# Routing, slots and scatter of two expert layers as one stage, zero rows written earlier, output stored by groups

## The reference, cut to what matters

```python
x = x + _L0_xattn_ref(_layernorm(x), ctx, ctx, ...)   # then L0_ffn, L1_xattn (performer)
x = x + _L1_ffn_ref(_layernorm(x, axis=-1), ...)      # 8 experts, two per row
x = x + _L2_xattn_ref(_layernorm(x), ctx, ctx, ...)   # keys of 16 heads x 64: ctx @ Wk
...                                                   # L2_ffn, L3_xattn
x = x + _L3_ffn_ref(_layernorm(x, axis=-1), ...)      # 8 experts, two per row

# the expert layers
logits = x @ Wg + bg                  # 8 logits a row
topk_vals, topk_idx = top_k(logits, 2)
weights = softmax(topk_vals)
out = sum of the two chosen experts' outputs, weighted
```

## Time and profile before

| | us |
|---|---|
| median of 3 runs | 3621.08 (3618.56 to 3623.73) |
| profiled execution | 3623.01 |
| its span | 3621.2 |
| L1f route and place | about 1380 to 1560 |
| L3f route and place | about 3131 to 3298 |
| last DVE instruction to the end | 15.7 |

### The profile page before, as it was taken

How to read it: one execution, slowest core, us unless ns; L and a number is a source line. 1 busy time by engine, 2 the same in 40 slices (tenths; PEclk the granted TensorE clock), 3 DMA queues, 4 the chain that set the end, 5 groups by cost and what they waited for, 6 DMA issues and landing times. The chain is left out here.

```text
span 3621.2 us, 73997 instructions
## 1 busy us (share of the span) xinstructions
PE 2969.1 (82%) x23917; PEld 2108.0 (58%) x23926; DVE 2351.7 (65%) x5338; ACT 1689.6 (47%) x2884; POOL 1213.0 (33%) x1311
## 2 busy tenths in 40 slices
PE   5997899999979996999959999984564999715980
PEld 4886222323227885889947777772343777515970
DVE  5887666666435657134458888859996898733653
ACT  3774788888934441423314444433443666300110
POOL 1112455555513441630013333320002777342005
PEclk9998899999989997999979999996786999857995
DMA  3000445445422004722232111100003333412224
GB/s 101 16 14 26 118 123 132 120 125 125 121 83 91 14 15 163 272 99 71 71 108 60 54 48 55 54 31 1 0 0 129 112 110 117 137 55 83 91 90 128
DMA packets 197370, 304.12 MB, mean 84 GB/s; under 512 B 23808, under 2 KB 134528, under 8 KB 191104
## 3 DMA queue, kind: packets, MB, share of 16 engines
q1 hardware_dynamic: 184816, 268.49, 24.1%
q0 software_dynamic: 12432, 34.10, 2.9%
HBM read 215.46 MB, written 78.64 MB: 81 GB/s over the span
## 5 line engine op out<-in xcount | busy, mean ns | idle before, releaser
L2308 ACT ACTIVATE params<-L0f_Z,params 128x1024 f32<-128x1024 f32 x512 | 532.6, 1113 | 84.0 <-PE L0f_Z L2364 83.8
L2285 POOL TENSOR_TENSOR L0f_mixed<-L0f_mixed,L0f_gated 128x512 f32<-128x512 f32 x240 | 332.0, 1383 | 291.7 <-DVE L0f_gated L2528 291.4
L2528 DVE SCALAR_TENSOR_TENSOR L0f_gated<-L0f_O,params 128x512 f32<-128x512 f32 x240 | 180.1, 750 | 223.9 <-PE L0f_O L2373 147.9
L2364 PE MATMUL L0f_Z<-params,L0f_w_stacked 128*128 128x512 f16 x1024 | 296.8, 388 | 34.1 <-ACT params L2308 23.3
L2373 PE MATMUL L0f_O<-params 128*32 128x512 f32 x2048 | 275.0, 609 | 0.4 <-ACT params L2308 0.4
L855 POOL TENSOR_TENSOR params<-params,L2x_recip_den 128x512 f32<-128x512 f32 x128 | 134.9, 1054 | 354.0 <-DVE L2x_recip_den L1110 353.6
L2364 PEld LDWEIGHTS L0f_Z<-params,L0f_w_stacked 128*128 128x128 f16 x1024 | 70.4, 98 | 289.9 <-ACT params L2308 266.2
L2008 ACT ACTIVATE L1ftiles_hidden<-L1ftiles_H,L1ftiles_b_tile 128x128 f32<-128x128 f32 x292 | 83.2, 368 | 196.3 <-PE L1ftiles_H L2031 196.3
L849 POOL DMA_INDIRECT L2x_gathered<-rows_out_dram,L1f_slots x64 | 63.8, 998 | 288.3 <-POOLq L136 256.3
L1554 DVE TENSOR_TENSOR L1x_products<-L1x_S,const_sb 128x512 f32<-128x512 f32 x128 | 82.5, 686 | 109.8 <-PE L1x_S L1464 109.8
L2031 PEld LDWEIGHTS L3ftiles_H<-L3ftiles_rowsT,L3ftiles_w_tile 128*128 128x128 f32 x1168 | 143.3, 195 | 7.4 <-DVE L3ftiles_rowsT L2059 2.0
(11 more groups left out here) (510 smaller groups left out, 7597.6 us busy)
## 6 DMA issues: line engine op xcount, KB each, us to landing
params<-gates_dram SPq DMA_DIRECT2D x512, 128.0 KB, 3.3
params<-side_dram SPq DMA_DIRECT2D x32, 1024.0 KB, 4.9
keysT_dram<-L1fplace_keysT SPq DMA_DIRECT2D x32, 512.0 KB, 3.4
params<-keysT_dram SPq DMA_DIRECT2D x32, 512.0 KB, 4.0
rows_in_dram<-L1froute_zero SPq DMA_DIRECT2D x2, 4864.0 KB
L1ftiles_rows<-rows_in_dram SPq DMA_DIRECT2D x76, 128.0 KB, 2.0
rows_in_dram<-L3froute_zero SPq DMA_DIRECT2D x2, 4864.0 KB
L3ftiles_rows<-rows_in_dram SPq DMA_DIRECT2D x76, 128.0 KB, 2.0
```

The lines of the kernel that those rows point to most:

```text
L2285: pool.tensor_tensor(acc[:, b.slot, m % KT, :], acc[:, b.slot, m % KT, :], tmp[:, m % 2, :], ALU.add).then_inc(mixed, 1)
L2308: act.activation(hid[:, n % 4, :, :], Z[:, n % 2, :, :], ACT.Gelu, bias=w["b1"][:, n // 4:n // 4 + 1]).then_inc(hid_ready, 1)
L2364: mm = pe.matmul(Z[:, n % 2, s, :], w1s[:, e, :], stack[:, b.slot, t, 2 * half + s, :], start=True, stop=True)
L2528: dve.scalar_tensor_tensor(out=out, in0=O[:, m % 2, :], scalar=w["b2"][:, e:e + 1], in1=gb[:, e % AHEAD, m % KT, :], op0=ALU.add, op1=ALU. ...
```

## The change

`route` and `place` become one stage, `prepare`. The norm's small steps are done once for all 32 batches instead of once for four. Routing goes in 16 turns of two batches; the rows' transposes of the next turn stand ahead of this turn's logits, and in L1f one key tile of L2x follows each turn from the fifth on (12 in all), four more stand ahead of the count. The applies write `kept` directly, so POOL's copies are gone. In L1f the gate's matmul takes 8 columns, in L3f 128 as before. The statistics of L1f's norm are taken in L1x, one instruction behind each `add_out`; those of L3f in its own stage. The zeros are written during L1x by 19 DMAs of four tiles, one behind a context load, and not at all before L3f. The key weights of L2x have a load and a semaphore of their own, issued second. The output is stored inside the combine stage, after each group of four batches.

```diff
--- before.py
+++ after.py
...
+    def load_columns(self, sp, phase, at, to, loaded):
+        sp.dma_start(self.stores[SIDE[phase]][:, at:to], self.dram["p_" + phase][:, at:to]).then_inc(loaded, 16)
...
-def last_stores(nc, sh):
-    stored = nc.alloc_semaphore("out_stored")
-    with nc.Block() as block:
-        @block.sync
-        def _(sp):
-            for q in range(4):
-                b = BATCH // 4
-                sp.dma_start(sh.dram["out"][q * b:(q + 1) * b].rearrange("b s d -> s b d"),
-                             sh.x[:, q * b:(q + 1) * b, :]).then_inc(stored, 16)
-            sp.wait_ge(stored, 64)
...
+        zero_set, zeroed, measured = core.sem("zero_set"), core.sem("slots_zeroed"), core.sem("rows_measured")
+        ZEROS, ZERO_TILES = 19, (SLOT_TILES + TILES_AHEAD) // 19
...
-            following(Turn(0, 2))
-            with sp.Fori(0, AHEAD) as i:
-                for s in (3, 4):
-                    following(Turn(i, s))
-            following(Turn(0, BATCH - 1))
+            tiles = sh.dram["rows_in"].rearrange("(j p) d -> p j d", p=P)
+            sp.wait_ge(zero_set, 1)
+            for b in range(2, BATCH):
+                following(Turn(0, b))
+                if 6 <= b < 6 + ZEROS:
+                    at = (b - 6) * ZERO_TILES
+                    sp.dma_start(tiles[:, at:at + ZERO_TILES, :],
+                                 zero[:, :].unsqueeze(1).broadcast_to([P, ZERO_TILES, D])).then_inc(zeroed, 16)
+            sp.wait_ge(zeroed, ZEROS * 16)
...
+            def measure(b):
+                dve.wait_ge(banks.emptied("proj"), banks.until_emptied("proj", b))
+                detach_wait(dve)
+                dve.bn_stats(sh.row_stats[:, b.n, :], sh.x[:, b.n, :]).then_inc(measured, 1)
...
                 if not first:
                     add_out(b.plus(-1))
+                    measure(b.plus(-1))
...
-        route(nc, sh, phase, w, c, kept, lg, rows_in, next_phase)
-        place(nc, sh, phase, c, lg[:, :, :], gate, slot, share, expert, kept, rows_in, next_phase)
+        prepare(nc, sh, phase, w, c, lg[:, :, :], gate, slot, share, expert, kept, rows_in, next_phase)
...
+def prepare(nc, sh, phase, w, c, lg, gate, slot, share, expert, kept, rows_in, next_phase):
...
+    E, G = 8, 2
...
+    measured = phase == "L1f"
+    keys_ahead = next_phase == "L2x"
+    LW = E if keys_ahead else P
...
+        xnT = core.sb("xnT", [P, KT, G * P])
+        X = core.ps("X", [P, 2, KT, G * P])
+        L = core.ps("L", [P, 2, BANK])
+        R, C = (X[:, k, :, :].rearrange("p k t -> p (k t)")[:, 0:BATCH * E] for k in range(2))
...
+        KEYS_FROM = 4
+        def keys_of(t):
+            return max(0, t - KEYS_FROM), max(0, t + 1 - KEYS_FROM)
+        ROUTE_KEYS = keys_of(TURNS)[0]
+        COUNT_KEYS = ROUTE_KEYS + 4
...
                 load(0)
+                sh.load_columns(sp, next_phase, KEY_COLUMNS, 2 * KEY_COLUMNS, wk_loaded)
                 load(1)
+                sh.loads[next_phase] = 32
+                for at in (0, 2 * KEY_COLUMNS):
+                    sh.load_columns(sp, next_phase, at, KEY_COLUMNS if at == 0 else columns(next_phase), sh.loaded[next_phase])
...
+            def empty_rows(t):
+                act.wait_ge(turned, t + 1)
+                if t:
+                    act.wait_ge(routed, t)
...
+            empty_rows(0)
+            for t in range(TURNS):
+                if t + 1 < TURNS:
+                    empty_rows(t + 1)
+                empty_keys(*keys_of(t))
...
+            def turn_rows(t):
+                pe.wait_ge(xn_ready, t + 1)
+                if t >= 2:
+                    pe.wait_ge(xT_ready, t - 1)
+                for k in range(KT):
+                    for j in range(G):
+                        mm = pe.transpose(X[:, t % 2, k, j * P:(j + 1) * P], kept[:, t * G + j, k * P:(k + 1) * P], c["ident"])
+                mm.then_inc(turned, 1)
+            def logits(t):
+                pe.wait_ge(xT_ready, t + 1)
+                if t >= 2:
+                    pe.wait_ge(logits_out, t - 1)
+                for j in range(G):
+                    for k in range(KT):
+                        mm = pe.matmul(L[:, t % 2, j * LW:(j + 1) * LW], xnT[:, k, j * P:(j + 1) * P], w["wg"][:, k, 0:LW],
+                                       start=(k == 0), stop=(k == KT - 1))
+                mm.then_inc(routed, 1)
+            def project_keys(first, end):
...
+            turn_rows(0)
+            for t in range(TURNS):
+                if t + 1 < TURNS:
+                    turn_rows(t + 1)
+                logits(t)
+                project_keys(*keys_of(t))
+            project_keys(ROUTE_KEYS, COUNT_KEYS)
...
+            def add_bias(t):
+                dve.wait_ge(routed, t + 1)
+                dve.tensor_tensor(lg[:, t * G:(t + 1) * G, :], L[:, t % 2, 0:G * LW].rearrange("p (j e) -> p j e", j=G)[:, :, 0:E],
+                                  w["bg"].unsqueeze(1).broadcast_to([P, G, E]), ALU.add).then_inc(logits_out, 1)
+            sh.wait_params(dve, phase)
+            norm_steps = Steps(dve, norm_step, 0)
+            if not measured:
+                for b in range(BATCH):
+                    last = dve.bn_stats(norm.stats[:, b, :], sh.x[:, b, :])
+                norm_steps.link(last)
+            norm.finish(dve, norm_steps)
+            for t in range(TURNS):
+                for b in range(t * G, (t + 1) * G):
+                    last = norm.apply(dve, kept[:, b, :], sh.x[:, b, :], b)
+                last.then_inc(xn_ready, 1)
+                if t >= 2:
+                    add_bias(t - 2)
+            add_bias(TURNS - 2)
+            add_bias(TURNS - 1)
+            dve.wait_ge(logits_out, TURNS)
...
+        stored = core.sem("out_stored")
...
+        @block.sync
+        def _(sp):
+            for t in range(TURNS):
+                rows = slice(t * G, (t + 1) * G)
+                sp.wait_ge(step, (t + 1) * 3)
+                sp.dma_start(sh.dram["out"][rows].rearrange("b s d -> s b d"), sh.x[:, rows, :]).then_inc(stored, 16)
+            sp.wait_ge(stored, TURNS * 16)
...
-        last_stores(nc, sh)
```

More of the change, by code:

```diff
@@ L78, with __init__ @@
     STEPS = 2 + RSQRT_STEPS
[L80 removed]
+    def __init__(self, core, group, name="ln", stats=None):
         self.group = group
[L82 removed]
+        self.stats = core.sb(name + "_stats", [P, group, 6]) if stats is None else stats
         self.mean_var = core.sb(name + "_mean_var", [P, group, 2])
@@ L1671, in experts_phase @@
     return Mixture(kept, slot, share, w) if relu else None
[L1674 to L1677 removed]
+def prepare(nc, sh, phase, w, c, lg, gate, slot, share, expert, kept, rows_in, next_phase):
+    E, G = 8, 2
     TURNS = BATCH // G
[L1679 to L1680 removed]
+    TILES = SLOT_TILES + TILES_AHEAD
+    measured = phase == "L1f"
+    keys_ahead = next_phase == "L2x"
+    LW = E if keys_ahead else P
     with ExitStack() as ctx:
[L1682 to L1729, removed]
[L1730 to L1773 removed]
@@ L1776, in place @@
-def place(nc, sh, phase, c, lg, gate, slot, share, expert, kept, rows_in, next_phase):
-    E = 8
-    TILES = SLOT_TILES + TILES_AHEAD
-    with ExitStack() as ctx:
-        core = Core(nc, ctx, phase + "place")
+        core = Core(nc, ctx, phase + "prepare")
+        norm = Norm(core, BATCH, stats=sh.row_stats)
         big = lambda name: core.sb(name, [P, BATCH, E])
-        rest, marks, chosen, place_, sums, more = (big(n) for n in ("rest", "marks", "chosen", "place", "sums", "more"))
+        rest, marks, chosen, place_, sums = (big(n) for n in ("rest", "marks", "chosen", "place", "sums"))
@@ L1784, in place @@
+        more = rest
         best, second, total = (core.sb(n, [P, BATCH]) for n in ("best", "second", "total"))
@@ L1837, in _, with empty_keys @@
         def _(act):
-            def empty_keys(n):
-                for t in range(KTILES):
-                    act.wait_ge(projected, KTILES * n + t + 1)
+            def empty_rows(t):
+                act.wait_ge(turned, t + 1)
+                if t:
+                    act.wait_ge(routed, t)
+                act.activation(xnT[:, :, :], X[:, t % 2, :, :], ACT.Copy).then_inc(xT_ready, 1)
+            def empty_keys(first, end):
+                for q in range(first, end if keys_ahead else first):
+                    n, t = q // KTILES, q % KTILES
+                    act.wait_ge(projected, q + 1)
                     if n >= 2 and t == 0:
                         act.wait_ge(keys_stored[n % 2], n // 2 * 16)
-                    act.activation(keys[:, n % 2, :, t, :], K[:, t, :].rearrange("p (j q) -> p j q", j=G), ACT.Copy,
+                    act.activation(keys[:, n % 2, :, t, :], K[:, t, :].rearrange("p (j q) -> p j q", j=KG), ACT.Copy,
                                    scale=0.125).then_inc(keys_out, 1)
-            if keys_ahead:
-                empty_keys(0)
+            empty_rows(0)
[3 more added lines that the diff above has]
+                empty_keys(*keys_of(t))
             act.wait_ge(centered, 1)
```

(20 more changed lines are left out.)

80 lines of the change are left out of this document (23 added, 57 removed).

## The result

The changed kernel takes **3586.49 us**, the median of 4 runs (3580.12 to 3587.51), against 3619.82 (3617.09 to 3623.73, 4 runs) beside it: ratio 0.990, 95% interval [0.989, 0.991]. The profiled execution takes 3586.45, its span is 3584.6. 3586 was predicted.

A forecast was written before the change was run, and what follows sets the result against it. L1f was taken as bound by routing, then PE's keys, with the scatter within 2 us; 0.4 - 21.1 - 5.2 - 9.5 = -35.4 takes 3623.0 to 3587.6, median 3586. Own range 3577 to 3600; overall 3567 to 3603.

The forecast's parts named there:

- L1x, +0.4: In L1x, statistics hide behind DVE's wait for PE and only the last shows, +0.4 us; the zeros cost nothing.
- sum: Whole kernel: 0.4 - 21.1 - 5.2 - 9.5 = -35.4 us.
- L1f routing, slots 5.6 earlier: In L1f, routing ends and slot arithmetic starts at 1433.0 instead of 1438.56.
- turns above 4 us: Sign that the forecast is wrong: routing turns above 4 us.
- a granted clock of 0.8 to 0.9: Sign for the forecast: PE's granted clock about 0.8 to 0.9 over L1f's routing.
- L1f stage, -21.1: L1f's keys end the stage at 1539.0, against 1560.14: -21.1 us.
- The scatter's end, 1537.8: In L1f, first scatter at 1452.7, 64 x 1.275 us and 3.5 to landing: 1537.8, within 2 us of the keys.
- L3f, -5.2: L3f's slots start at 3184.7 instead of 3189.93: -5.2 us, bounds -11.6 and +4.4, four parts of ten cold.
- warm rival: PE warm throughout: L1f's stage 29.7 us earlier, L3f's 11.6 earlier, sum -50.4, 3571; chance 0.25.
- 0.25 of hand-overs: Routing turns where ACT and PE alternate: 0.60 + 0.25 of hand-overs + 0.95 = 1.8 us warm.
- The end, -9.5: Kernel's end: only 0.5 MB is stored behind the last addition, 15.75 - 6.2 = -9.5 us, bounds -12 and -6.
- cold rival: PE cold throughout routing: L1f's stage +0.1 us, L3f +4.4, sum -4.6, 3616, no change; chance 0.07.

The follow-up runs named there:

- experiment 5: Changed kernel with the statistics of L1f's norm moved from L1x back to the head of L1f; median 3593.2, ratio 0.992 to the kernel before.
- experiment 8: Changed kernel with 128-column gate in L1f, seven key tiles ahead of the count, keys stored in pairs, two transposed-row buffers in L3f; 3565.5, ratio 0.984 to kernel before.
- experiments 3: Changed kernel with a key tile behind every turn of L1f's routing from turn 0, 16 instead of 12; median 3582.3, ratio 0.989 to the kernel before.
- experiment 10: Changed kernel with the four edits of experiment 8 and L3f's statistics taken in L3x; median 3553.0, ratio 0.981 to the kernel before.
- experiment 6: Changed kernel with the output again stored by four 1 MB DMAs in a stage of its own at the end; median 3592.2, ratio 0.992 to kernel before.
- experiments 1: Changed kernel with L1f's gate products taking 128 columns instead of 8; median 3576.3, ratio 0.987 to the kernel before.
- 2: Changed kernel with L3f's gate products taking 8 columns instead of 128; median 3590.3, ratio 0.991 to the kernel before.
- 11: Changed kernel with L3f's gate products taking 128 columns in turns 0 to 5 and 8 columns behind them; 3587.8, one execution.
- experiment 4: Changed kernel with no key tile in L1f's routing, four ahead of the count and 124 behind it; median 3591.3, ratio 0.991 to the kernel before.
- 9: Changed kernel with the statistics of L3f's norm taken in L3x, one instruction behind each addition to x; 3572.4, ratio 0.987 to the kernel before.
- experiment 7: Changed kernel with the zeros moved from L1x to the head of L1f's queue, two 5 MB DMAs ahead of the key weights; 3589.7, ratio 0.991 to kernel before.

## Why the prediction was right, point by point

- **L1x, +0.4**: right. The statistics are hidden (experiment 5), and the zeros too: from the first normalized row to the last addition L1x takes 301.6 us in the kernel before and 301.7 in the changed one. The last statistics show, 2.1 us instead of 1.6 from that addition's start to the next stage. The sum counts this term twice: the 1539.0 of L1f already starts from the later 1381.2.
- **L1f routing, slots 5.6 earlier** (6.2 counted from the stage's start): 6.4 on that count. Two errors cancelled, which is luck. I took a quarter of the later turns cold, and half of the first four; in fact all of the first four were and nearly four of the twelve others, 29.8 us at 0.50, for a reason the prediction didn't have. Against it stood warm turns of 2.20 for which I took 2.35, and first turns that cost 2.63 cold and not 2.8. Two of the prediction's own signs tell it: turns above 4 us were named as wrong, and four took 4.27; a granted clock of 0.8 to 0.9 was named as right, and it was 0.68 from PE's first transpose to the slot arithmetic.
- **L1f stage, -21.1**: the mis-sized term; -16.7. Routing and the removed wait for the exponential came as said. From the stage's start to the next one 157.8 us were forecast and 162.9 measured, 5.1 more. Missing from the sum were PE's 2.31 us ahead of the counts, where the key tiles that stood ahead of them (4.56 us in the profile) were too few for DVE's 6.4 us, and 112 tiles at 0.890 instead of 0.864 (2.9 us), most of it the fall of the clock behind that pause: the first 32 took 29.5, 1.8 more than at 0.865. In experiment 8 both are gone.
- **The scatter's end, 1537.8**: wrong, without effect here. I took 3.5 us from the last issue to the end; it is 8.6, and the kernel before shows that in L3f, where nothing else ends the stage (last issue 3289.9, next stage 3298.4). By it the chain ends at 1543.1, 3 us before the next stage starts behind the keys, and it sets the end in experiments 3, 8 and 10 (10.1, 9.4 and 8.7 us behind the last issue).
- **L3f, -5.2**: -9.4, near the warm rival's -11.6: two cold turns, not four in ten. A warm turn took 1.90 and not 1.8; no row shows the 0.25 of hand-overs in that 1.8, and PE waited 0.31 for ACT's copy in each.
- **The end, -9.5**: -11.3; confirmed by experiment 6 and, that the stores lie under the gathers, too.
- The **sum** -35.4 came out as 36.6 less span. The shortfall of L1f (4.4) is made up by L3f (4.2) and the end (1.9). The start of L1x was 2.1 later by chance, and L3f's tiles stage, whose code is the same, 2.1 shorter (219.3 instead of 221.4; 221.1 again in experiment 10). That 3586 was met to half a microsecond is luck, for errors of 2 to 4 us cancelled. The mechanisms were right but for three: the clock, PE's cover ahead of the counts, and the scatter's end.
- The **cold rival** was worked out for both stages from rows of before. In L1f's first 29 us it was true, in L3f not. The Trainium skill, "TensorE: Matmul & The Clock Gate" (Part 4, PE-mode transpose), on whose rule I based it, doesn't explain this: transposes are a third of every turn in L3f, where the clock was 1.00 from the third turn on. What tells the cases apart is the width of the gate products (experiments 1, 2 and 11).

## What to carry to other kernels

Before a stage is filled with small products, look at the granted clock beside PE's busy share. Here PE was busy 100% at 0.50 with gate products of 8 columns; padded to 128 they cost nothing and made routing 9.6 us shorter. When an engine's work is moved under a wait, read the idle time just ahead of the instruction that follows it; 0.7 us a turn sufficed for 0.55. And count what runs out first ahead of a wait (here four key tiles against 6.4 us): the pause costs itself and, in most profiles here, the clock behind it.

## What the runs showed of the hardware

- With products of 128x128 by 8 columns and transposes between them TensorE stayed at 1.2 GHz for 40 us while PE was busy without a pause (experiment 4), and fell from 2.4 within 5 us (11, one execution); with 128 columns the same turns were up after 6 us (1). Eight of them take 1.88 us cold and 0.96 warm; with 128 columns 2.07 and 1.06.
- A pause of 2.3 to 2.4 us of PE was followed by a fall of the clock in the changed kernel and in experiments 1, 2, 5, 9 and 11, not in 3, 6 and 7, where the same instructions stand around it: the lengths of this stage differ by up to 4.5 us between profiles of one code (162.9 and, in experiment 6, 158.4).
- In experiment 7 a DMA of 5.0 MB (4864 KB), the second of two, landed after 28.4 us, and the issue of the 256 KB one behind it took 12.6 us.
